# GpSimd takes the low halves of the normed rows and the sums of the key and query features in the attention steps

## The reference

```
x = x + linear_attention(layernorm(x), W)
x = x + cross_attention(layernorm(x), ctx, ctx, Wq, bq, Wk, bk, Wv, bv)
x = x + mixture(layernorm(x))        # shared expert + 8 experts, top 2, hidden 1024

linear_attention(x, W):
    q, k, v = split(x @ W);  q = elu(q) + 1;  k = elu(k) + 1
    KV = sum_l k_l^T v_l;  Z = 1 / (q . sum_l k_l + 1e-6)
    return (q @ KV) * Z
layernorm(x): (x - mean) / sqrt(var + 1e-5)
```

## Time and profile before

| | |
|---|---|
| median of three runs | 774.11 us (773.34 to 774.57) |
| span of the profiled execution | 771.6 us |
| PE busy | 739.3 us, 96% |
| DVE busy | 593.3 us, 77% |
| ACT busy | 413.6 us, 54% |
| POOL busy | 228.5 us, 30% |
| chain that ended last | PE 88%, DVE 4%, DMA 4%, ACT 1% |
| PE idle in the stretch 200 to 220 us | 4.3 of 20 us |

### The profile page before, as it was taken

One profiled execution on the slowest core, in us unless ns is written; L12 is line 12 of the kernel. 1 busy time (PEld: TensorE's weight loads), 2 busy tenths in 40 slices (PEclk: granted clock), 3 DMA queues, 4 the chain that ended last, 5 costly groups with the idle time before them and its releaser, 6 DMA issues.

```text
span 771.6 us, 21959 instructions
## 1 busy us (share of the span) xinstructions
PE 739.3 (96%) x6919; PEld 617.6 (80%) x6919; DVE 593.3 (77%) x1796; ACT 413.6 (54%) x936; POOL 228.5 (30%) x221
## 2 busy tenths in 40 slices
PE   3999999999888999999999999999999999999995
PEld 2677677777677888888888888888888888878783
DVE  4589999998868889999776667667667777777774
ACT  4577667666776666766633333333333334555552
POOL 2110110110110257666212333332333333333333
PEclk9999999999999999999999999999999999999998
DMA  5666987874372179998724443455544443444541
GB/s 148 173 169 162 225 207 181 215 151 83 78 198 84 59 234 314 306 295 265 202 60 71 70 66 57 64 66 68 71 64 59 65 67 66 73 74 73 72 66 21
DMA packets 163123, 97.29 MB, mean 126 GB/s; under 512 B 105260, under 2 KB 158408, under 8 KB 163016
## 3 DMA queue, kind: packets, MB, share of 16 engines
q1 hardware_dynamic: 149720, 78.81, 42.1%
q0 software_dynamic: 13296, 17.09, 13.0%
HBM read 38.73 MB, written 36.15 MB: 97 GB/s over the span
## 4 chain that ended last, share of the span: by engine, by line
PE 88%; DVE 4%; DMA 4%; ACT 1%; SPq 1%; issue 1%; POOL 0%; DVEq 0%; ACTq 0%; POOLq 0%
PE bank_kv L1389 9%; PE bank_kv L1390 9%; PE bank_kv L1391 9%; PE bank L1366 6%; PE bank L1368 6%; PE bank L1367 6%; PE bank_st L1368 6%; PE bank_st L1366 6%; PE bank_st L1367 6%; PE bank_kv L1487 5%; PE bank_kv L1382 5%; PE bank_st L1466 4%; PE bank_st L1447 3%; PE bank L1494 3%; PE bank_kv L1383 2%; DMA w_parts<-w_parts 1%
## 5 line engine op out<-in xcount | busy, mean ns | idle before, releaser
L1389 PE MATMUL bank_kv<-w_parts,expert_buffers 128*128 (+1 forms) x656 | 179.0, 273 | 2.9 <-DVE expert_buffers L1009 2.9
L748 ACT ACTIVATE expert_buffers<-bank_st,bias_columns 128x256 f32<-128x256 f32 (+1 forms) x248 | 108.2, 437 | 136.8 <-DVE expert_buffers L1009 77.7
L1391 PE MATMUL bank_kv<-w_parts,expert_buffers 128*128 (+1 forms) x656 | 179.0, 273 | 0.0
L1390 PE MATMUL bank_kv<-w_parts,expert_buffers 128*128 (+1 forms) x656 | 178.9, 273 | 0.0
L748 ACT ACTIVATE expert_buffers<-bank,bias_columns 128x256 f32<-128x256 f32 (+1 forms) x246 | 107.2, 436 | 128.6 <-PE bank L1368 97.9
L1009 DVE SCALAR_TENSOR_TENSOR expert_buffers<-expert_buffers 128x256 f16<-128x256 f32 x328 | 138.9, 425 | 22.6 <-ACT expert_buffers L754 13.0
L1008 DVE TENSOR_SCALAR expert_buffers<-expert_buffers 128x256 f16<-128x256 f32 x260 | 82.3, 316 | 62.9 <-ACT expert_buffers L748 55.6
L668 POOL DMA_INDIRECT out<-expert_buffers,token x71 | 117.3, 1652 | 18.7 <-issue 18.5
L1366 PE MATMUL bank<-expert_buffers,w_parts 128*128 128x256 f16 (+1 forms) x368 | 87.0, 248 | 0.7 <-ACT expert_buffers L748 0.7
L1368 PE MATMUL bank_st<-expert_buffers,w_parts 128*128 128x256 f16 (+1 forms) x368 | 87.1, 249 | 0.0
L1368 PE MATMUL bank<-expert_buffers,w_parts 128*128 128x256 f16 (+1 forms) x368 | 87.1, 249 | 0.0
(11 more groups left out here) (214 smaller groups left out, 1559.0 us busy)
## 6 DMA issues: line engine op xcount, KB each, us to landing
rows_by_expert<-w_parts SPq DMA_DIRECT2D x12, 795.0 KB, 5.4
stage_w<-in_L_ffn_Wfc SPq DMA_DIRECT2D x9, 512.0 KB, 5.4
stage_w<-in_L_ffn_Wproj SPq DMA_DIRECT2D x9, 512.0 KB, 5.7
rows<-in_x SPq DMA_DIRECT2D x16, 256.0 KB, 4.9
x_residual<-rows SPq DMA_DIRECT2D x16, 256.0 KB, 2.5
expert_buffers<-x_residual SPq DMA_DIRECT2D x16, 256.0 KB, 3.7
out<-expert_buffers SPq DMA_DIRECT2D x16, 256.0 KB, 5.0
w_parts<-in_L_ffn_Wfc SPq DMA_DIRECT2D x7, 512.0 KB, 5.9
```

The costliest lines, as they stand in the source:

```text
L748: act.activation(spare[:, at], hid_of(c)[:, 0:width(G)], ACT.Gelu_apprx_tanh, bias=bias, scale=UNSCALE).then_inc(s["gelu_done"], 1)
L1389: pe.matmul(y, g[:, 0, tile(t)], w_hi, start=f == 0 and t == 0, stop=False, skip_group_check=True)
L1390: pe.matmul(y, g[:, 0, tile(t)], w_lo, start=False, stop=False, skip_group_check=True)
L1391: op = pe.matmul(y, g[:, 1, tile(t)], w_hi, start=False, stop=f == FC - 1, skip_group_check=True)
```

## The change

Four things move or are rewritten.

1. The normed rows come out 16 times as large: DVE's variance instruction multiplies var + eps by 1/256, so that the power gives 16 rstd. ACT's high parts are then a plain rounding, and the low part is a subtraction of two tensors.
2. The low parts of all three norms in the steps are issued by POOL (new lines 611, 616 and 620). Only three stay on DVE: the very first of norm one, and those of norm three for blocks 14 and 15.
3. The feature sums of keys and queries are issued by POOL, each as two instructions: a minimum with 1 in place, and an addition that waits for it over a new semaphore `clamped` (lines 624, 627, 629, 632).
4. POOL's loop is written out in full. In a step it takes low two (i-2), low three (i-4), low one (i+1), keys, queries, then the power. DVE's `layer_norm` now waits for the low part of the block before in place of the high part, and its `shift` instruction gets a wait for `hi1_ready`.

The core of the diff:

```
+                if live(i - 2):
+                    got(pool, "hi2_ready", i - 2)
+                    pool.tensor_tensor(halves16[1][:, :, 1, :], xn[1], halves16[1][:, :, 0, :], ALU.subtract)\
+                        .then_inc(s["lo2_ready"], 1)
+                if live(i - 4) and i <= LAST + 2:
+                    b = i - 4
+                    got(pool, "hi3_ready", b)
+                    pool.tensor_tensor(rows16[:, b * TB:(b + 1) * TB, D:2 * D], xn[2], rows16[:, b * TB:(b + 1) * TB, 0:D],
+                                       ALU.subtract).then_inc(s["lo3_ready"], 1)
+                if live(i + 1) and i != -1:
+                    got(pool, "hi1_ready", i + 1)
+                    pool.tensor_tensor(halves16[0][:, :, 1, :], xn[0], halves16[0][:, :, 0, :], ALU.subtract)\
+                        .then_inc(s["lo1_ready"], 1)
+                if live(i):
+                    got(pool, "expk_ready", i)
+                    pool.tensor_scalar(expk, expk, 1.0, None, ALU.min).then_inc(s["clamped"], 1)
+                    got(pool, "reluk_ready", i)
+                    pool.wait_ge(s["clamped"], 2 * i + 1)
+                    pool.tensor_tensor(kfeat, expk, kfeat, ALU.add).then_inc(s["kfeat_ready"], 1)
...
-                act.activation(halves16[n][:, :, 0, :], xn[n], ACT.Copy, scale=A_SCALE).then_inc(s[f"hi{n + 1}_ready"], 1)
+                act.activation(halves16[n][:, :, 0, :], xn[n], ACT.Copy).then_inc(s[f"hi{n + 1}_ready"], 1)
...
-                got_if(dve, f"hi{n + 1}_ready", b - 1)
+                got_if(dve, f"lo{n + 1}_ready", b - 1)
...
-                if live(i - 2):
-                    low(1, i - 2)
-                if live(i - 4):
-                    low_third(i - 4)
...
-                if live(i + 1) and i != -1:
-                    low(0, i + 1)
...
-                    dve.scalar_tensor_tensor(kfeat, expk, 1.0, kfeat, ALU.min, ALU.add).then_inc(s["kfeat_ready"], 1)
...
-                    dve.scalar_tensor_tensor(qfeatT, expq, 1.0, qfeatT, ALU.min, ALU.add).then_inc(s["qfeat_ready"], 1)
```

More of the change, by code:

```diff
@@ L351, in apart @@
             eng.wait_ge(s["ones_set"], 1)
[L353 to L361, removed]
         SPLIT_STEPS = {3: (1, 0), 5: (2, 0), 7: (1, 1), 9: (2, 1)}
@@ L618, in step @@
             def step(i):
[L619 to L625, removed]
+                if live(i - 2):
[17 more added lines that the diff above has]
+                    pool.tensor_tensor(kfeat, expk, kfeat, ALU.add).then_inc(s["kfeat_ready"], 1)
+                    got(pool, "expq_ready", i)
+                    pool.tensor_scalar(expq, expq, 1.0, None, ALU.min).then_inc(s["clamped"], 1)
+                    got(pool, "reluq_ready", i)
+                    pool.wait_ge(s["clamped"], 2 * i + 2)
+                    pool.tensor_tensor(qfeatT, expq, qfeatT, ALU.add).then_inc(s["qfeat_ready"], 1)
+                pool.wait_ge(s["var_ready"], i + 3)
+                pool.tensor_tensor(rstd[:, :], var_eps[:, :], minus_half[:, :], ALU.pow)\
+                    .then_inc(s["rstd_ready"], 1)
+            for i in range(-2, LAST + 4):
+                step(i)
             pool.wait_ge(s["logits_done"], B)
@@ L718, in high_third @@
                 act.wait_ge(s["x2_stored"], (b + 1) * 16)
-                act.activation(rows16[:, ds(b * TB, TB), 0:D], xn[2], ACT.Copy, scale=A_SCALE)\
-                    .then_inc(s["hi3_ready"], 1)
+                act.activation(rows16[:, ds(b * TB, TB), 0:D], xn[2], ACT.Copy).then_inc(s["hi3_ready"], 1)
             def copy_prob(b):
@@ L892, in layer_norm, with low_first @@
                 op.then_inc(s[f"xn{n + 1}_ready"], 1)
[L894 to L898, removed]
+            def low_first():
+                got(dve, "hi1_ready", 0)
+                dve.tensor_tensor(halves16[0][:, :, 1, :], xn[0], halves16[0][:, :, 0, :], ALU.subtract)\
+                    .then_inc(s["lo1_ready"], 1)
             def split_shared(which, half, chunk):
@@ L969, in low_third @@
                 got(dve, "hi3_ready", b)
-                dve.scalar_tensor_tensor(rows16[:, ds(b * TB, TB), D:2 * D], xn[2], A_SCALE,
-                                         rows16[:, ds(b * TB, TB), 0:D], ALU.mult, ALU.subtract)\
-                    .then_inc(s["lo3_ready"], 1)
+                dve.tensor_tensor(rows16[:, ds(b * TB, TB), D:2 * D], xn[2], rows16[:, ds(b * TB, TB), 0:D],
+                                  ALU.subtract).then_inc(s["lo3_ready"], 1)
             def invert_sum(b):
@@ L995, in variances @@
                 chain(op, "stats_step", i + 3)
-                dve.tensor_scalar(var_eps[:, :].rearrange("p (n t) -> p n t", n=3), mv[:, :, :, 1], LN_EPS, None,
-                                  ALU.add).then_inc(s["var_ready"], 1)
+                dve.tensor_scalar(var_eps[:, :].rearrange("p (n t) -> p n t", n=3), mv[:, :, :, 1], LN_EPS,
+                                  1.0 / (A_SCALE * A_SCALE), ALU.add, ALU.mult).then_inc(s["var_ready"], 1)
             def split(c):
@@ L1024, in step @@
                     layer_norm(0, 0)
-                    low(0, 0)
+                    low_first()
                     for k in range(DK):
@@ L1031, in step @@
                 elif live(i + 1):
+                    got(dve, "hi1_ready", i)
                     dve.scalar_tensor_tensor(shift[:, :], mv[:, 0, :, 0], -1.0, rstd[:, 0:TB], ALU.mult, ALU.mult)\
```

6 lines of the change are left out of this document (1 added, 5 removed).

## The result

The changed kernel takes **787.37 us** (median of four runs, 786.53 to 790.35) where the kernel before took 773.73 beside it: a ratio of 1.0174, 95% interval 1.0158 to 1.0190. It is slower by 13.6 us. The direction was forecast, the size was not: 776.9 had been given, with 784 as the upper end.

A forecast was written before the change was run, and what follows sets the result against it. PE with its chain was the bound, DVE adding 0.23 us in eight steps. -1.84 + 2.39 + 2.22 = +2.77 us on the 771.6 us span gives 774.4, plus 2.5 makes 776.9 us; range 772.5 to 784.

The forecast's parts named there:

- it fits, if the order of its waits lets it: POOL's work per attention step: 5 x 1.25 + 2 x 0.88 + 1.32 = 9.3 us of 11.67, taken to fit.
- the end of the path: POOL's power, last in its step, ends at 185.9 and DVE wants it at 186.9: cost nothing.
- The mis-sized term: Price of POOL's minimum over 512 columns in the feature sums: 0.88 us, from the affine select's one read stream.
- it is long: Rival: POOL's two-input instructions take 1.5 us, low three is 1.45 us later, every step pays: 783.5 us, chance 0.15.
- The gain: DVE gets room for the 0.67 us weight split, so eight periods go from 11.90 to 11.67 us: 1.84 us.
- The port rival: Rival: DVE's two-input instructions and POOL's hold each other up, delaying the weight split: +7.8, 781.9 us, chance 0.05.
- The turns: Transposing DMAs behind low three, 0.95 us later: 2.39 us in steps 8, 10, 15 and 2.22 us in 16, 17.
- near steps: Steps 8, 10 and 15, whose transposing DMAs had 0.2 us or nothing to spare: 2.39 us together.
- I keep the number of them: Steps with long transposing DMAs: their number stays as before the change, though which steps get them is unknown.
- The key sum: POOL's key sum before the state product: 0.63 us to spare, nothing; in the first two steps at worst a few tenths.

The follow-up runs named there:

- the split placed clear: Kernel before with only the eight weight splits on GpSimd, multiplication behind low three and subtraction behind the key sum, both ahead of the power: 773.35 us, ratio 0.9985.
- sums alone: Changed kernel with the three low parts back on VectorE, so GpSimd makes only the key and query sums: 780.80 us, ratio 1.0077.
- the split on GpSimd: Kernel before with only the eight weight splits on GpSimd, two instructions each behind its power, its loop unrolled: 776.98 us, ratio 1.0030.
- the low parts alone: Changed kernel with the key and query sums back on VectorE, so GpSimd makes only the three low parts: 779.46 us, ratio 1.0066.
- the run with nothing moved: Kernel before with norms giving rows times 16 and GpSimd's loop unrolled, all low parts and sums still on VectorE: 774.82 us, ratio 1.0004.
- the run with low three first: Changed kernel with low three ahead of low two in GpSimd's step: 787.26 us, ratio 1.0168.

## Why the prediction was wrong

**The failed step** is the sentence "it fits, if the order of its waits lets it", which put the wait around POOL's queue at nothing, with its counterpart at the end of the path: the power "ends at 185.9, wanted at 186.9: nothing". The busy time of POOL, 9.3 us, was set against 11.67 as if the rest were free. But POOL works in order, and its last instruction releases, through DVE and ACT, its first. Walked around, with my own prices, the ring is 9.3 + 1.51 from the power to low two + 0.2 for the handovers to the additions = 11.0 us (the 1.51 as measured after the change): it would have fitted, with some 0.6 us to spare that I had not worked out. The end of the path says the same once it is read right: norm two began 3.55 us behind the state product, so in step 15 the power was wanted at 183.01 + 3.55 = 186.6, not 186.9, 0.6 us behind its end at 185.9. And that time I read off a trace in which DVE was held by the score maximum; with POOL late, DVE is held by POOL. What the runs show in place of "nothing" is a ring of 12.06 us that PE has to follow.

**The mis-sized term** is the minimum. The streams of the affine select gave 0.88 us; it takes 1.49, and some 1.64 from its start to that of the addition, where I had 0.98. Twice 0.65 us, less 0.3 since the subtractions are shorter than I took them, turn the ring of 11.0 into 12.06 us. Without the minimum the kernel comes to 777.4 us, near the 776.9 that I had forecast; that is luck rather than a confirmation, since its ten steps lose 1.5 us where my terms up to there give 0.55. The same streams had given 1.25 us for the two-input instructions: measured 1.09 to 1.16 for the subtractions and 1.27 for the additions, well inside the bounds I set. So the rival "it is long", nearest in number with 783.5, did not have the mechanism: its long instructions were these.

**The gain**, 8 x 0.23 us, was right as a fact of the kernel before: the split placed clear shows 1.86. In the changed kernel it could not come, since PE no longer decided; there the split costs 3.9 us on the ring.

**The port rival**, at 0.05, had the right mechanism at the wrong place. I judged it by the power, which ran beside DVE's query sum with no loss on either side. There the power had begun first. Where a split was already running, the power too took 1.80 us in place of 1.35 (sums alone), and at 512 columns the two hold each other up in many rows. The clash takes 3.9 us here, and it is what made the split on GpSimd slower than before.

**The turns.** That low three comes later and that near steps pay was right in kind. Low three ends 174.59 + 1.13 - 173.47 = 2.25 us after low two begins, 2.33 after the end of high two, against 1.65: 0.7 us later, less than the 0.95 put down; and yet the low parts alone cost 5.1 us where 1.4 were expected of that delay. The step that failed is "I keep the number of them": with 0.3 us left to the logits (1.0 less 0.7), landings that the kernel before absorbed are waited for. With the low parts alone PE waits for turned rows eleven times from 60 to 245 us, where before it was four and I had counted on five.

**The key sum** "at worst a few tenths" in the first steps: PE waited 1.45 us in the first one for the key sum and 0.95 for the query sum, where before it had waited 0.32 and 0.69 us for ACT, and 0.84 us for the key sum of step 3. From step 2 to step 3 it is 11.02 us where before, and without the minimum, it is 10.02. The loss by step 5 is 3.0 us, some 0.5 of which may be chance.

**The clock.** From 180 us on the changed kernel's windows show, last columns clock, DMA share and GB/s:

```profile
185.00:190.00 5.00, 5.00 (x39) 3.25 (x37) 2.69 (x12) 4.82 (x11) 4.30 (x4) 1.00 0.13 26
190.00:195.00 5.00, 3.27 (x37) 2.64 (x34) 3.20 (x13) 1.30 (x5) 4.70 (x5) 0.90 0.77 154
195.00:200.00 5.00, 5.00 (x33) 3.55 (x33) 1.93 (x7) 2.41 (x8) 1.25 (x2) 0.76 0.30 48
215.00:220.00 5.00, 2.97 (x33) 1.91 (x32) 3.68 (x15) 1.71 (x7) 1.32 (x1) 0.79 0.64 139
220.00:225.00 5.00, 4.98 (x34) 3.52 (x35) 2.50 (x9) 4.92 (x13) 1.34 (x2) 0.53 0.10 36
```

```profile
193.08 0.46 PE L1435 MATMUL bank<-w_parts 128*128 128x8 f16 x12 [1.73 <-DMA w_parts<-rows]
193.39 3.21 PE L1447 MATMUL bank_st<-w_parts 128*128 128x257 f32 x8
```

The granted clock of the first row, 1.00, is the upper of the two levels, 2.4 GHz; that of the last, 0.53, is near the lower one, 1.2 GHz, and the rows between mix both. PE had waited 1.73 us for a turn just before the drop, and the state product behind it takes 3.21 us in place of 1.98. Before, these stretches had 1.00. What the clock cost in all was not measured apart: about 1.2 us in this product, and part of the 2.8 us behind step 15. Other profiles show such a dip only behind 200 us, that of the run with nothing moved too (0.90 and 0.76 from 215 to 225 us); the run with low three first has none up to 230 us.

What stays open: how the changed kernel's last 2.8 us divide between the clock, the longer turns and the ring, and why some turns take 4 us to land (of the third turn's the median is 2.5); no run took these apart.

## What to carry to other kernels

An engine that "fits" by its busy time can still set the pace: walk its queue once around, from the last instruction through everything that it releases on other engines back to the first, add the idle time on that way, and compare the sum with the period. When work is given to an idle engine, read which instructions of the busy one run beside it, and put it where those don't hold it up and it doesn't hold them: the same two instructions made the kernel 2.7 us slower in one place, and in another they cost nothing and shortened the ten steps by 1.9 us. And a chain whose time to spare before a DMA's landing is less than the spread of the landings, here 2.4 to 4.0 us for the third turn, should be counted as used up.

## What the runs showed of the hardware

- On POOL an instruction with one input and a constant, 512 columns of fp32 in place, takes 1.49 us (minimum) or 1.50 us (multiplication); an addition of two such inputs takes 1.27 us and a subtraction into fp16 1.09 to 1.16 us. One input is not cheaper than two. The Trainium skill, "GPSIMD Engine Reference", section 4.1, calls one-input work there "roughly line-rate"; on VectorE the 256 columns of a norm took 0.41 us, so 512 would be some 0.8, an estimate from that row, and the measured 1.49 does not agree. The estimate of 1.12 us from its section 3.1 for two inputs lies near the measured prices.
- Six memsets of one column, 96 ns each by their group, delay what follows by only 0.20 us together.
- A POOL instruction over 512 columns holds up even VectorE instructions of 2 columns until it ends: 0.15 became 1.12 us. The power, with 6 columns, is itself held by a VectorE split that began before it: 1.35 became 1.80 us.
